# Picking 4 of 28 columns on TensorE in the first multi-head pass of a graph network

## The reference

```python
q = (h @ Wq[i]).reshape(n, H, dh)          # D = 64, H = 4 heads, dh = 16
k = (h @ Wk[i]).reshape(n, H, dh)
v = (h @ Wv[i]).reshape(n, H, dh)
scores = jnp.einsum('ehd,ehd->eh', q[dst], k[src]) / jnp.sqrt(jnp.float32(dh))
scores = scores + e @ We[i]                # e: 32 features of each edge
m = jax.ops.segment_max(scores, dst, num_segments=n)
p = jnp.exp(scores - m[dst])
denom = jax.ops.segment_sum(p, dst, num_segments=n)
alpha = p / (denom[dst] + 1e-09)
agg = jax.ops.segment_sum((alpha[:, :, None] * v[src]).reshape(-1, D), dst, num_segments=n)
h = _ln(h + agg @ Wo[i], gn[i], bn[i])
emsg = jax.nn.gelu(jnp.concatenate([h[src], h[dst], e], axis=-1) @ Wem[i] + bem[i])
e = _ln(e + emsg, ge[i], be[i])
```

## Time and profile before

| | us |
|---|---|
| median of 3 runs | 10206.79 (10204.67 to 10208.48) |
| the profiled execution: its own time | 10210.79 |
| its span, first to last instruction | 10209.0 |
| POOL busy in the span | 7477.5 (73%) |
| DVE busy | 7363.6 (72%) |
| PE busy | 6617.0 (65%) |
| ACT busy | 5584.2 (55%) |
| mean granted TensorE clock | 0.789 of full speed |

### The profile page before, as it was taken

How to read it: one execution, slowest core, us unless ns; L and a number is a source line. 1 busy time by engine, 2 the same in 40 slices (tenths; PEclk the granted TensorE clock), 3 DMA queues, 4 the chain that set the end, 5 groups by cost and what they waited for, 6 DMA issues and landing times. The chain is left out here.

```text
span 10209.0 us, 106412 instructions
## 1 busy us (share of the span) xinstructions
PE 6617.0 (65%) x29219; PEld 5572.4 (55%) x29219; DVE 7363.6 (72%) x13024; ACT 5584.2 (55%) x6064; POOL 7477.5 (73%) x7352
## 2 busy tenths in 40 slices
PE   6888878859978996996997688621114333343333
PEld 5776767748867885885886577621113222232222
DVE  8777666657766775776777799845554788858887
ACT  2555556657766775775776456523332455535553
POOL 7888867767767776776776777677776777677774
PEclk8899879979988997997998688855555666656665
DMA  6544433322322332332454355434443555545553
GB/s 226 92 81 81 77 94 79 81 63 74 87 79 59 89 85 52 87 89 64 117 142 131 102 136 139 117 107 131 131 139 100 181 184 188 168 131 183 184 188 101
DMA packets 792292, 1183.93 MB, mean 116 GB/s; under 512 B 472967, under 2 KB 547571, under 8 KB 784515
## 3 DMA queue, kind: packets, MB, share of 16 engines
q0 software_dynamic: 322752, 363.08, 17.9%
q1 hardware_dynamic: 405373, 470.66, 15.1%
q10 hardware_dynamic: 64070, 349.10, 8.5%
HBM read 733.35 MB, written 461.77 MB: 117 GB/s over the span
## 5 line engine op out<-in xcount | busy, mean ns | idle before, releaser
L1165 POOL DMA_INDIRECT turned<-d_t,idx x5788 | 5483.2, 947 | 1823.8 <-issue 1753.3
L1310 PE MATMUL banks<-pair,hot 128*128 128x462 f32 x16184 | 3479.9, 376 | 185.1 <-DVE wide L1431 139.0
L1310 PEld LDWEIGHTS banks<-pair,hot 128*128 128x128 f32 x16184 | 3059.3, 190 | 604.7 <-DVE wide L1431 204.5
L1366 PE MATMUL banks<-ident,wide 128*128 128x128 f32 x588 | 160.5, 417 | 1585.0 <-ACT wide L1185 867.4
L928 ACT ACTIVATE hot<-keys,row 128x1024 fp32r<-128x1024 f32 (+1 forms) x1036 | 1073.4, 1117 | 150.4 <-PE banks L1310 72.8
L847 POOL DMA_INDIRECT d_acc<-work,idx x560 | 956.2, 1707 | 194.1 <-issue 165.3
L1641 DVE TENSOR_TENSOR_SCAN wide<-banks,wide 128x224 f32<-128x224 f32 (+4 forms) x1288 | 1037.5, 872 | 5.8
L1366 PEld LDWEIGHTS banks<-ident,wide 128*128 128x128 f32 x588 | 101.0, 209 | 1660.7 <-ACT wide L1185 897.9
L1279 ACT COPY wide<-wide 128x952 f32<-128x952 f32 (+2 forms) x252 | 502.4, 1994 | 844.1 <-DVE wide L1641 844.1
L939 ACT ACTIVATE hot<-hot 128x3584 fp32r<-128x3584 f32 (+1 forms) x296 | 907.7, 3115 | 0.6
L1431 DVE TENSOR_TENSOR wide<-banks,member 128x462 f32<-128x462 f32 x1156 | 670.4, 633 | 284.2 <-PE banks L1310 251.0
(11 more groups left out here) (352 smaller groups left out, 9790.7 us busy)
## 6 DMA issues: line engine op xcount, KB each, us to landing
d_e<-wide ACTq DMA_DIRECT2D x168, 924.0 KB
turned<-d_t,idx POOLq DMA_INDIRECT x5788
d_e<-wide ACTq DMA_DIRECT2D x84, 1008.0 KB
wide<-d_b SPq DMA_DIRECT2D x60, 1344.0 KB
keys<-d_key SPq DMA_DIRECT2D x124, 512.0 KB, 4.0
keys<-d_edge_key SPq DMA_DIRECT2D x203, 256.0 KB, 4.5
d_b<-wide SPq DMA_DIRECT2D x28, 1344.0 KB, 8.7
wide<-d_edge SPq DMA_DIRECT2D x84, 448.0 KB, 6.3
```

The lines of the kernel that those rows point to most:

```text
L1165: gp.indirect_dma_start(rows[:, b, k, :], None, table[:, :], offset(idx[:, b, k:k + 1])).then_inc(s["gathered"][b], 16)
L1310: mm = nc.tensor.matmul(ps_cols[i], hot[:, place, i, j, :], flat(g.pair[:, part, j]), start=(j, part) == (0, 0), stop=(j, part) == (SETS - ...
```

## The change

The first multi-head pass picks 4 of its 28 columns on TensorE (`MULTI_COLS = 4`, `cols=MULTI_COLS`), and GpSimd gathers 24.

- A column goes through two PSUM banks, 3 and 7, one for each half row (`ps_half`). `ring_columns` computes half h of a column after VectorE has taken half h of the one before (`cols_taken`), and `ring_take` multiplies and sums each half by itself.
- One-hots are built per column (`column_hot`) in a ring of two slots. Column i waits until the column two before it is done. In a chunk ScalarE builds columns 2 and 3 after the message product, and columns 0 and 1 of the chunk after next's number (`chunk + 3`) after the state copies, as the last thing in a chunk.
- TensorE's body is new (`with_picks`): turn, product, then the four columns of the next chunk. The product is split: 128 columns into banks 1 and 2, and 16 columns of logits into the free end of bank 2, with the same weights, so 14 matmul calls for 7.
- VectorE takes column 0 after the factors, column 1 after the value product, columns 2 and 3 after the scans. The scans of line 1641 have a quarter of a head's features (`FR = HF // 4`): 16 of 112 elements.
- The node step ahead uses the layout of the one before the dot pass (`lent=True`): the table part goes through a ring of three (`kf`) and is split into `pair` group by group on VectorE (`split_set`), three operations of 896 elements each. It no longer copies `x` to `h`; `g.h` holds the keys, the mask and the queries' rows in the pass, and GpSimd copies `x` to `h` at the pass's end.
- SP loads the keys of a chunk after its fourth one-hot.

```diff
 AHEAD = 2
+MULTI_COLS = 4
+HOT_RING = 2
@@ Picks
+        if self.ring:
+            self.keys = g.h[:, K:K + 2 * X, :].rearrange("p (x a) e -> p x a e", a=2)
+            self.member = g.h[:, K + 2 * X:K + 3 * X, 0:SET]
+            self.hot = ph.sbuf("hot", [P, HOT_RING, SETS, P], F32R)
+            self.pair = ph.sbuf("pair", [P, 2, SETS, KF, SET], F32R)
+            return
@@
+def column_hot(nc, g, act, pk, n, i, slot, first=False):
+
+    q = pk.X * (n - 1) + i
+    if not first:
+        act.wait_ge(pk.s["cols_done"], 2 * (q - 1))
+    act.wait_ge(pk.s["keys_loaded"], 16 * n)
+    for j in range(SETS):
+        last = nc.scalar.activation(pk.hot[:, slot, j, :].rearrange("p (a e) -> p a e", a=2), pk.keys[:, i], ACT.Abs,
+                                    bias=g.row[:, j * SET:j * SET + 1], scale=-1.0)
+    last.then_inc(pk.s["hot_link"], 1)
+    act.wait_ge(pk.s["hot_link"], q + 1)
+    part = pk.hot[:, slot].rearrange("p s e -> p (s e)")
+    nc.scalar.activation(part, part, ACT.Relu, bias=1.0, scale=-1.0).then_inc(pk.s["hot_made"], 1)
@@ edges
-        FR = HF // 2
+        FR = HF // 4 if ring else HF // 2
@@ gpsimd
+        if ring:
+            gp.wait_ge(s["b_turned"], CHUNKS + 2)
+            gp.wait_ge(picks["cols_taken"], 2 * X * CHUNKS)
+            nc.gpsimd.tensor_copy(g.h, g.x).then_inc(s["h_kept"], 1)
+            gp.wait_ge(s["h_kept"], 1)
@@ scalar
+            if ring and (more or b == 0):
+                for i in range(HOT_RING, X):
+                    column_hot(nc, g, act, pk, chunk + 2, i, (X * (b + 1) + i) % HOT_RING)
...
+            if ring and more:
+                for i in range(HOT_RING):
+                    column_hot(nc, g, act, pk, chunk + 3, i, (X * (b + 2) + i) % HOT_RING)
@@ tensor
+        def ring_columns(n, b, first=False):
+
+            for i in range(X):
+                q = X * (n - 1) + i
+                pe.wait_ge(picks["hot_made"], q + 1)
+                for h in range(2):
+                    if not first or i:
+                        pe.wait_ge(picks["cols_taken"], 2 * (q - 1) + h + 1)
+                    for j in range(SETS):
+                        for part in range(2):
+                            mm = nc.tensor.matmul(ps_half[h], hot[:, (X * b + i) % HOT_RING, j, :],
+                                                  flat(pk.pair[:, part, j, h * HALF:(h + 1) * HALF, :]),
+                                                  start=(j, part) == (0, 0), stop=(j, part) == (SETS - 1, 1))
+                    mm.then_inc(picks["cols_done"], 1)
@@
+        def with_picks(t, b, more):
+
+            chunk = 2 * t + b
+            pe.wait_ge(s["e_loaded"][b], 16 * (t + 1))
+            turn(chunk, b)
+            pe.wait_ge(s["em_copied"], chunk + 1)
+            for i, (q0, q1) in enumerate(HALVES):
+                for q in range(q0, q1):
+                    if q % 4 == 0:
+                        pe.wait_ge(s["e_copied"], 2 * chunk + q // 4 + 1)
+                    nc.tensor.matmul(ps_em[:, i, (q - q0) * P:(q - q0 + 1) * P], e_T[:, q, :], w_cat[:, 16:],
+                                     start=True, stop=True)
+                    mm = nc.tensor.matmul(ps_logits[:, 16 * q:16 * q + 16], e_T[:, q, :], w_cat[:, 0:16],
+                                          start=True, stop=True)
+            mm.then_inc(s["we_product"], 1)
+            if more or b == 0:
+                ring_columns(chunk + 2, b + 1)
@@ vector
+        def ring_take(n, buf, i, link):
+
+            q = X * (n - 1) + i
+            if i == 0:
+                link(nc.vector.tensor_tensor(member, mid(g.iota[:, 0:SET], X),
+                                             bc(g.in_set[:, n + AT - 1, PICKED - X:], SET), ALU.is_equal))
+            for h in range(2):
+                v.wait_ge(picks["cols_done"], 2 * q + h + 1)
+                nc.vector.tensor_tensor(found, ps_half[h].rearrange("p (w c) -> p w c", c=SET),
+                                        mid(member[:, i], HALF), ALU.mult).then_inc(picks["cols_taken"], 1)
+                v.wait_ge(picks["cols_taken"], 2 * q + h + 1)
+                link(nc.vector.tensor_reduce(rows[:, buf, KG + i, h * HALF:(h + 1) * HALF], found, AX.X, ALU.add))
@@ nodes, build
-            if pk is not None and gat and j >= late:
+            if pk is not None and not summing and j >= late:
                 split(j - late)
...
-        layer(nc, g, dict(kind="dot", rows=g.x, copy=g.h, weights=a["l3_w0"], extra=True, out_w=192,
+        layer(nc, g, dict(kind="dot", rows=g.x, lent=True, weights=a["l3_w0"], extra=True, out_w=192,
                           tables=[(g.d_t128, 0, 128), (g.d_q64, 128, 192)], spread=(g.d_b64, 128, 192),
-                          seed=(g.d_q64, D)), dict(kind="multi", a=w_edges(0)))
+                          seed=(g.d_q64, D)), dict(kind="multi", a=w_edges(0), ahead=0, cols=MULTI_COLS))
```

More of the change, by code:

```diff
@@ L1055, in edges @@
             ps_cols = [banks[:, 2 * (i % 2):2 * (i % 2) + 2, 0:SET * HALF] for i in range(X)]
+        elif ring:
+            ps_half = [banks[:, i, 0:SET * HALF] for i in (3, 7)]
         else:
@@ L1073, in edges @@
     THIRDS = [(i, q, min(q + 3, G4)) for i, q in enumerate(range(0, G4, 3))]
+    ps_logits = banks[:, 2, 3 * P:3 * P + 16 * G4]
     def product(i, q0, q1):
         return ps_both[:, i, 0:(q1 - q0) * (16 + P)].rearrange("p (q x) -> p q x", x=16 + P)
-    em_rows, em_out = (tiles[n] for n in ("em_rows", "em_out")) if multi else (None, None)
+    em_rows = tiles["em_rows"] if multi and not ring else None
+    em_out = tiles["em_out"] if multi else None
     norm = ps_em.rearrange("p a x -> p (a x)")[:, 0:K * DE].rearrange("p (k f) -> p k f", f=DE)
@@ L1103, in _ @@
                 sp.dma_start(gs[:], a["e_norm"].partition_broadcast(P)).then_inc(s["loaded"], 16)
-        for n in range(2, 2 if not X else 3 if dot else AH + 4):
+        if ring:
+            sp.wait_ge(picks["hot_made"], X)
+            sp.dma_start(keys, step_keys(g, X, 2 + AT).rearrange("p (x a e) -> p x a e", a=2, e=P // 2)
+                         ).then_inc(picks["keys_loaded"], 16)
+        for n in range(2, 2 if not X or ring else 3 if dot else AH + 4):
             sp.wait_ge(picks["hot_made"], HB * (n - 1))
@@ L1215, in _ @@
         act.dma_start(prime[0:1, 0:1], g.d_x[0:1, 0:1]).then_inc(s["stored"], 16)
-        for n in range(2, AH + 3 if X and not dot else 2):
+        for n in range(2, AH + 3 if X and kind == "gat" else 2):
             one_hots(nc, g, act, pk, n, n % 2, n == 2)
@@ L1223, in _ @@
             act.dma_start(prime[0:1, 4:5], g.d_x[0:1, 0:1]).then_inc(s["em_stored"][0], 16)
+        for i in range(HOT_RING, X if ring else 0):
+            column_hot(nc, g, act, pk, 1, i, i % HOT_RING)
         act.wait_ge(s["state_init"], 1)
@@ L1254, in one @@
                 copy_logits(chunk)
-            if X and not dot and more:
+            if kind == "gat" and more:
                 one_hots(nc, g, act, pk, chunk + AH + 3, (b + AH + 1) % 2)
@@ L1405, in _ @@
         join_tails()
-    LINKS = {"gat": 6, "dot": 12, "multi": 17 if update else 11}[kind] + (1 + X if dot else 3 if X else 0)
+    LINKS = {"gat": 6, "dot": 12, "multi": 17 if update else 11}[kind] + (1 + X if dot else 1 + 2 * X if ring else 3 if X else 0)
     @block.vector
@@ L1444, in _ @@
                 wide_take(1, 0, i, link)
-        if not X or dot:
+        if ring:
+            link = Link(v, s["first_link"])
+            for i in range(X):
+                ring_take(1, 0, i, link)
+        if not X or dot or ring:
             v.wait_ge(ready["spread_done"], 16 * C)
@@ L1615, in one @@
             nc.vector.tensor_copy(maxima[:, :, 0:1], maxima[:, :, K:K + 1])
-            if X and not dot and (more or b == 0):
+            if ring and (more or b == 0):
+                ring_take(chunk + 2, 1 - b, 0, link)
+            if kind == "gat" and (more or b == 0):
                 take(chunk + AH + 2, 1 - b, KG, 0, EARLY, link)
@@ L1626, in one @@
                 wide_take(chunk + 2, 1 - b, 1, link)
+            if ring and (more or b == 0):
+                ring_take(chunk + 2, 1 - b, 1, link)
             if update:
@@ L1649, in one @@
                 wide_take(chunk + 2, 1 - b, 3, link)
-            elif X and (more or b == 0):
+            elif ring and (more or b == 0):
+                for i in range(2, X):
+                    ring_take(chunk + 2, 1 - b, i, link)
+            elif kind == "gat" and (more or b == 0):
                 take(chunk + AH + 2, 1 - b, KG, EARLY, X, link)
@@ L1957, in first_hots @@
         def first_hots():
+            if pk.ring:
+                for i in range(HOT_RING):
+                    column_hot(nc, g, act, pk, 1, i, i, True)
+                return
             if pk.wide:
```

73 lines of the change are left out of this document (55 added, 18 removed).

## The result

| | before | after |
|---|---|---|
| median of the runs (4 each, same chip) | 10205.73 us | 10305.85 us |
| lowest to highest | 10200.33 to 10208.48 | 10302.21 to 10318.15 |
| ratio after / before, 95% | | 1.0101 [1.0086, 1.0116] |
| profiled execution: time, span | 10210.8, 10209.0 | 10304.11, 10301.9 |
| granted clock, mean of the span | 0.789 | 0.818 |

The change costs 100 us. It is slower, as forecast, and inside the range (10195 to 10315), but by more than twice the 46 us that were forecast.

The account below looks back on a forecast made before the run. GpSimd's 28 gathers, 35.03 us a chunk, bound the first multi-head pass. VectorE starting at 6787.0 plus 27 chunks of 36.9, less the old last start 7738.0, plus 0.4, gave +45.7 us: median 10253, range 10195 to 10315.

Parts of the forecast that it names:

- GpSimd stops being the bound: First multi-head pass: 24 gathers take GpSimd 30.0 us a chunk, under VectorE's 32.9, so GpSimd no longer sets the pace.
- rival 4: First multi-head pass: gathers slow beside more traffic, step 1.25 to 1.46 us, so GpSimd isn't freed; under 2%.
- VectorE's work: VectorE's chunk in the multi-head pass grows from 21.65 to 32.9 us without waits, mostly 10.56 for taking columns.
- Column 3's wait: After the scans VectorE waits 1.06 and 1.5 us for column 3's halves from TensorE, making its cycle 35.5 us.
- The ring: Chain through VectorE, TensorE and ScalarE from one chunk's scans to the next's sets the pace, 36.9 us; chance 0.52.
- The clock: TensorE runs the edge product at the low clock (6.1 us) after a pause, the columns behind it high (5.68).
- Rival 1: VectorE alone sets the multi-head pass's pace, 35.5 us a chunk; +8 us, 10215; chance 0.20.
- Rival 2: TensorE's clock falls in column bursts too, +3.0 us a column; chunk 38.4 to 39.9, +86 to +127 us; chance 0.18.
- Rival 3: TensorE's halves run ahead of VectorE, so its wait goes; chunk 32.9 us, total 10145 (-62); chance 0.09.
- The node step: Ahead of the pass, seven splits (24 to 48 us of VectorE) hide beside 91 us of GpSimd; 0, at most +5.
- Around it: Work beside the chunks is hidden, such as GpSimd's new 3136-element copy, 3.8 us; twice as slow and bare, +7.6.

Follow-up runs that it names:

- e1: Changed kernel with column 1's one-hot built behind the edge-feature turn instead of ahead of it; 10259.98 us, 1.0067 of the kernel before.
- e3: Changed kernel with the product's seven 16-column logit matmuls made one of 112 columns (edge logits wrong in value); 10259.59 us, 1.0066 of the kernel before.
- a1: Changed kernel again, unedited, on the chip of the experiments; 10317.10 us, 1.0106 of the kernel before.
- e2: Changed kernel plus 12 idle matmuls of 448 columns a chunk ahead of the four transposes; 10259.36 us, 1.0068 of the kernel before.
- e10: Changed kernel plus 12 idle matmuls ahead of the transposes and 9 more ahead of column 3; 10267.40 us, 1.0056 of the kernel before.
- e9: Changed kernel, four columns, with both one-hots behind the turn and column 2's take between the scans; 10181.38 us, 0.9975 of the kernel before.
- e4: Changed kernel with three columns instead of four (MULTI_COLS = 3), same layout; 10249.64 us, 1.0057 of the kernel before.
- e8: Changed kernel with three columns and the one-hots of columns 0 and 1 both behind the turn; 10096.85 us, 0.9912 of the kernel before.
- e5: Changed kernel with column 1's one-hot behind the turn and column 2's take between the 8th and 9th scan; 10255.52 us, 1.0065 of the kernel before.
- e7: Changed kernel with only column 2's take moved between the 8th and 9th scan; 10337.63 us, 1.0146 of the kernel before.

## Why the prediction was right and wrong

- **GpSimd stops being the bound**: right, and shown by its releaser. The step of a gather stayed at (471.5 + 146.0) / 499 = 1.24 us without its waits, so rival 4 is out.
- **VectorE's work**: forecast 32.9, measured 33.1 to 33.3. Takes step 0.66 to 0.70 as forecast, 16 scans took 4.58 (4.63). What was left out is some 0.4 on the mean, a gap of 0.7 at the head of every second chunk (L1609).
- **Column 3's wait**: 1.06 + 1.5 forecast, 1.14 + 1.56 where the clock was high.
- **The ring**: right in its course and in four of its six terms, by the table above. e1 and e3 each took one link out and c fell by 1.6.
- **The clock** is the step that failed: "the product falls into the low part and the columns behind it into the high one". The first half held (product at 0.50, 7.15 us with its copy and transposes for 7.4). The second did not. Column 0 began at 0.50 and ran at it for 4.8 and 2.5 us in the two chunks, +1.73 us on the mean of two chunks; column 3 began low in every second one, which with a smaller excess in the other makes +0.92. Of these 2.65 the other terms give 0.3 back, and on the mean of all chunks 2.2 are left: 27 x 2.2 = 59 us. With the node step's 7.3, and less the 10.8 and the 8.0 by which unchanged code ahead and behind was shorter in this execution, that is the 48 us between the forecast and the profiled execution (10304.1 - 10256.5). The 19 us of unchanged code didn't come again: in a1's profile the dot pass's last gather starts at 6581.2, as in the kernel before, and beside the kernel before of its own set a1 lies 111 us higher, 65 over the forecast of 46, near the 59 and the 7.3 together. The mistake was in reading: there the clock rose some 6 us after a start with columns, and the forecast let the product's 6.1 us stand for these 6. Here it rose 9 and 11 us after TensorE resumed with transposes and product, but 3 us after it resumed with a column (7204.65): the product didn't stand for columns. e2 shows that this is a cause and not a companion: more work for TensorE, less time.
- **Rival 1** (35.5): not seen. With the columns' waits at 2.7 a chunk of e10 takes 36.4 to 36.5, and one without the 0.7 gap would by estimate take some 35.5 (the second chunk's 38.63 less its waits for columns of 5.88, and 2.7): 36.0 on the mean is this rival's place, 0.5 above its price.
- **Rival 2** was half the truth: "the clock falls in the column bursts too" holds for column 3 in every second chunk, and the measured 39.1 lies between its 38.4 and 39.9. But its price of 3.0 a column was twice what column 3 showed (1.43), and the larger loss, at column 0, was in no rival. The Trainium skill (TensorE: Matmul & The Clock Gate, A second HAM failure mode: psum-queue depth-cycling) tells of a clock that falls and rises between groups that cycle through PSUM banks, and of the throughput that this costs; the trace agrees, with two falls in the chunk of 38.63 us and a mean clock of 0.83 in the pass. The rival deserved more than 0.18.
- **Rival 3** (faster): it asked for ring waits under 2.3 us. e9 gets them down to 0.87 with four columns, and lies 25 us under before; but by another order, which the change doesn't have.
- **The node step** is the second step that failed: "Worth 0; if that cover of 91 us is short, at most +5". The splits themselves took 30.0 us of VectorE (12.5 + 12.3 + 5.2), inside the 24 to 48; but GpSimd, which was to hide them, was held by their subtractions, and the node step grew by 7.3 us, 7.7 in a1. No run took the splits out, so the cause rests on which of the DMAs were long.
- **Around it**: the first idx copy 31.4 after the first gather as forecast; GpSimd's copy 2.79 us (3.8), with 41.7 of waiting ahead of it, hidden.

Left open: what in the small instructions of 16 columns keeps the clock low. e3, which took 12 of 14 out, shows that the late rise goes with them and not with the pause or the transposes; it also shortened the product, and no run changed their number or size alone.

## What to carry to other kernels

When an engine's share is lightened by giving work to three others that hand it round, sum the ring link by link, and price each burst at the clock that the burst before it leaves; a product of small matmuls behind a pause may not bring the clock back. Then look at what stands ahead of the ring's link in an in-order engine's program: moving two one-hots behind one copy was worth 5.7 us a chunk (e4 to e8), more than the column itself. And a wait that vanishes from one place (e5, e7) is worth nothing until the whole ring is shorter. Last, work that lies beside a busier engine can still lengthen that engine's own work, as the splits did.

## What the runs showed of the hardware

- Twelve idle matmuls of 448 columns a chunk made the kernel some 0.33% faster (e2), with a granted clock of 0.93 in the pass instead of 0.83.
- A 28-instruction product of 128 and 16 columns takes 3.05 us at 1.00 (7193.87 to 7196.92 in e1) and 5.83 at 0.50 (7216.42 to 7222.25 in the changed kernel); a column of 28 matmuls of 448 takes 5.98 to its last hand-off at 1.00 and 7.1 to 8.2 where it starts at 0.50.
- The length of a pause alone doesn't decide whether the clock falls. In the changed kernel it fell in the pause of 2.63 us ahead of 7204.65 and not in that of 2.53 ahead of 7243.28; but in e2 it stayed at 1.00 in pauses of 2.62 (ahead of 7183.04) and 2.72 us.
- The clock came back 2.9 to 6.1 us after the transposes in e3 and 9.0 to 11.8 us in the changed kernel, whose product has 12 more instructions of 16 columns.
- An indirect DMA of GpSimd's that began while VectorE subtracted two SBUF tensors of 896 elements (L992) took 1.74 to 2.45 us, all seven of them; beside VectorE's operations on one tensor (L990, L991) it took 0.94 to 0.96 with two exceptions, in the changed kernel's node step.
- GpSimd's copy of 3136 fp32 elements a row took 2.79 us, 0.89 ns an element, for the 1.22 of VectorE's multiply in the earlier trace rows.
